# Splitting the second projection and the third residual of a fused attention block into column halves

## The reference

```
x = x + 0.5 * ffn(layernorm(x))
x = x + attn(layernorm(x))
x = x + 0.5 * ffn(layernorm(x))

ffn(u)  = u @ sign(weight).T
attn(u): Q = phi(u @ Wq.T + bq); K = phi(u @ Wk.T + bk); V = u @ Wv.T + bv     (16 heads of 64)
         KV = sum over n of K^T V;  Z = sum over n of K
         out = (Q KV) / (Q Z + eps);  return out @ Wo.T + bo
phi(a) = elu(a) + 1
```

## Time and profile before

| | us |
|---|---|
| median of three executions | 2138.48 |
| lowest and highest of them | 2082.67, 2271.7 |
| the profiled execution | 2096.74 |
| span of its slowest core, core 7 | 2095.1 |
| spans of the other seven cores | 2070.2 to 2080.0 |

### The profile page before, as it was taken

One profiled execution on the slowest core, in us unless ns is written; L12 is line 12 of the kernel. 1 busy time (PEld: TensorE's weight loads), 2 busy tenths in 40 slices (PEclk: granted clock), 3 DMA queues, 4 the chain that ended last, 5 costly groups with the idle time before them and its releaser, 6 DMA issues.

```text
span 2095.1 us, 33065 instructions; the slowest of 8 cores (2070.2 to 2095.1 us)
## 1 busy us (share of the span) xinstructions
PE 1771.3 (85%) x10784; PEld 793.9 (38%) x10784; DVE 759.3 (36%) x2049; ACT 1230.2 (59%) x2025; POOL 147.5 (7%) x274
## 2 busy tenths in 40 slices
PE   0499898998998998989989999878888888888887
PEld 0233333333333333333333333334444444444443
DVE  2133333333333333333333333134434444444443
ACT  1467667767667777676776766634444444444443
POOL 1000000000000001000000000010110011011010
PEclk9999999999999999999999999989999999999999
DMA  8622222222222223222222221123332332333332
GB/s 180 122 86 69 88 66 88 89 66 88 89 66 87 79 76 118 77 76 89 65 87 81 75 88 56 60 86 117 126 116 111 127 116 111 126 116 113 125 120 83
DMA packets 134630, 199.34 MB, mean 95 GB/s; under 512 B 88384, under 2 KB 88384, under 8 KB 134464
## 3 DMA queue, kind: packets, MB, share of 16 engines
q0 software_dynamic: 32960, 109.08, 15.5%
q1 hardware_dynamic: 101504, 88.15, 13.5%
HBM read 104.87 MB, written 83.89 MB: 90 GB/s over the span
## 4 chain that ended last, share of the span: by engine, by line
PE 64%; ACT 20%; issue 9%; DVE 4%; DMA 3%; ACTq 1%; DVEq 0%; SPq 0%
PE pA L465 43%; PE pA L476 12%; PE pA L470 3%; DVE y3t L323 3%; ACT mnb L399 3%; ACT mxb L401 3%; PE pA L480 2%; ACT kbQ L387 2%; ACT eb L400 2%; ACT u2fm L437 2%; PE tpB L455 2%; ACT kbQ L388 1%; DMA y3t<-wfT 1%; DMA stg<-wfT 1%; ACT kbK L403 1%
## 5 line engine op out<-in xcount | busy, mean ns | idle before, releaser
L476 PE MATMUL pA<-wv,u1fm 128*128 128x512 bf16 x1024 | 258.0, 397 | 97.2 <-ACT kbK L403 97.2
L465 PE MATMUL pA<-wo,attnfm 128*128 128x512 bf16 x1024 | 235.4, 383 | 70.6 <-DVE y3t L323 57.6
L465 PE MATMUL pA<-sw,u2fm 128*128 128x512 bf16 x1024 | 231.2, 379 | 48.0 <-ACT u2fm L439 44.3
L476 PE MATMUL pA<-wk,u1fm 128*128 128x512 bf16 x1024 | 242.4, 379 | 18.3 <-ACT kbQ L387 18.3
L465 PE MATMUL pA<-sw,u0fm 128*128 128x512 bf16 x1024 | 235.1, 383 | 0.0
L465 PE MATMUL pA<-wq,u1fm 128*128 128x512 bf16 x1024 | 232.1, 380 | 0.0
L437 ACT COPY u2fm<-tpB 128x512 bf16<-128x512 bf16 x64 | 37.5, 586 | 298.2 <-PE tpB L455 298.2
L476 PEld LDWEIGHTS pA<-wv,u1fm 128*128 128x128 bf16 x1024 | 93.4, 100 | 222.1 <-issue 137.7
L384 ACT ACTIVATE u2b<-y1t 128x1024 bf16<-128x1024 f32 x63 | 66.6, 1058 | 185.2 <-DVE y1t L283 185.2
L314 DVE TENSOR_TENSOR phiQ<-eb,mxb 128x1024 bf16<-128x1024 bf16 x64 | 44.3, 692 | 344.6 <-ACT mxb L401 344.6
L465 PEld LDWEIGHTS pA<-wo,attnfm 128*128 128x128 bf16 x1024 | 96.6, 98 | 183.8 <-issue 80.4
(11 more groups left out here) (120 smaller groups left out, 2454.8 us busy)
## 6 DMA issues: line engine op xcount, KB each, us to landing
xt<-x SPq DMA_DIRECT2D x64, 512.0 KB, 3.9
y1scr<-y1t POOLq DMA_DIRECT2D x64, 512.0 KB, 3.9
y1in<-y1scr POOLq DMA_DIRECT2D x64, 512.0 KB, 3.6
out<-y3t SPq DMA_DIRECT2D x64, 512.0 KB, 2.6
qscr<-qfm POOLq DMA_DIRECT2D x64, 256.0 KB, 3.2
qfin<-qscr POOLq DMA_DIRECT2D x64, 256.0 KB, 3.8
qfm<-phiQ SPq DMA_TRANSPOSE x512, 2.3
stg<-wfT SPq DMA_DIRECT2D x4, 512.0 KB, 8.7
```

Source lines behind the costliest of these rows:

```text
L465: mm = e.matmul(dst[:, h*512:(h+1)*512], lhs_fm[:, c*P:(c+1)*P], w_sb[:, c, h*512:(h+1)*512], start=(c == 0), stop=(last and c == 7))
L476: mm = e.matmul(dst[:, h*512:(h+1)*512], lhs_fm[:, c*P:(c+1)*P], w_sb[:, c, h*512:(h+1)*512], start=(c == 0), stop=(last and c == 7))
```

## The change

FFN and Wo of stage 2 no longer go through `proj`. Each is written out with the column half h as the outer loop, so the first half of `pA2` is complete after 8 matmuls. `tFfn2` counts halves. L323 becomes two instructions of 512 columns, each waiting for its half and each counting in `vY3`. Wo waits for the `y3t` half of the bank that it is about to write. Each of the two products now waits once, ahead of its first matmul, for both half copies of its input (`sU2fm`, `sAttnfm`). Wo's bias matmul comes at the end of each half. Thresholds of `tFfn2` and `vY3` elsewhere are doubled.

```
@@ VectorE
-                    v.wait_ge(tFfn2, t - 2)
+                    v.wait_ge(tFfn2, 2 * t - 5)
                     if tf >= 2:
                         v.wait_ge(dY3o[tf % 2], 16 * (tf // 2))
-                    v.scalar_tensor_tensor(y3t[:, tf % 2, :], pA2[:, :], 0.5, y2t[:, tf % 2, :],
+                    v.scalar_tensor_tensor(y3t[:, tf % 2, 0:512], pA2[:, 0:512], 0.5,
+                                           y2t[:, tf % 2, 0:512],
+                                           ALU.mult, ALU.add).then_inc(vY3, 1)
+                    v.wait_ge(tFfn2, 2 * t - 4)
+                    v.scalar_tensor_tensor(y3t[:, tf % 2, 512:1024], pA2[:, 512:1024], 0.5,
+                                           y2t[:, tf % 2, 512:1024],
                                            ALU.mult, ALU.add).then_inc(vY3, 1)
@@ TensorE
                     if t > NT:
-                        e.wait_ge(vY3, t - 3)
-                    proj(e, u2fm[:, (t - 3) % 2, :], sw, pA2[:, :], None, tFfn2,
-                         cw=(sU2fm, 2 * t - 5))
+                        e.wait_ge(vY3, 2 * (t - 3))
+                    e.wait_ge(sU2fm, 2 * t - 4)
+                    for h in range(2):
+                        for c in range(8):
+                            mm = e.matmul(pA2[:, h*512:(h+1)*512],
+                                          u2fm[:, (t - 3) % 2, c*P:(c+1)*P],
+                                          sw[:, c, h*512:(h+1)*512], start=(c == 0),
+                                          stop=(c == 7))
+                        mm.then_inc(tFfn2, 1)
@@
-                    if t >= 3:
-                        e.wait_ge(vY3, t - 2)
-                    proj(e, attnfm[:, (t - 1) % 2, :], wo, pA2[:, :], bor, tWo,
-                         cw=(sAttnfm, 2 * t - 1))
+                    e.wait_ge(sAttnfm, 2 * t)
+                    for h in range(2):
+                        if t >= 3:
+                            e.wait_ge(vY3, 2 * t - 5 + h)
+                        for c in range(8):
+                            e.matmul(pA2[:, h*512:(h+1)*512],
+                                     attnfm[:, (t - 1) % 2, c*P:(c+1)*P],
+                                     wo[:, c, h*512:(h+1)*512], start=(c == 0), stop=False)
+                        mm = e.matmul(pA2[:, h*512:(h+1)*512], ones_row[0:1, :],
+                                      bor[0:1, h*512:(h+1)*512], start=False, stop=True)
+                    mm.then_inc(tWo, 1)
```

More of the change, by code:

```diff
@@ L186, in _ @@
                 s, j = t // NJ, t % NJ
-                e.wait_ge(vY3, t + 1)
+                e.wait_ge(vY3, 2 * (t + 1))
                 if t >= 2:
@@ L337, in _ @@
                     if 3 <= t <= NT + 2:
-                        v.wait_ge(vY3, t - 2)
+                        v.wait_ge(vY3, 2 * (t - 2))
                     v.wait_ge(tWo, t)
```

## The result

| | before | after |
|---|---|---|
| median of the executions, us | 2084.54 (10 runs) | 2119.93 (9 runs) |
| profiled execution, us | 2096.74 | 2125.11 |
| span of core 7 in it, us | 2095.1 | 2123.4 |
| after / before | | 1.0178, 95% interval 1.0165 to 1.0191 |

The changed kernel is 1.8% slower, 35 us by the medians. That is far outside the scatter of the measurement, though under 2%. The forecast was +27 us, 1.3%. By it the kernel before has 2077 to 2080 us and the changed one 2113.5, give or take 1 us.

What follows compares the result with a forecast made beforehand. The loop through `pA2` (Wo, `y2t`, FFN, `y3t`) was taken to bound, ScalarE's loop close behind; +0.42 us in 62 iterations gave +26.0, iterations 1 and 2 +1.4, together +27.4: 2124.1 us, range 2094 to 2156.

Steps and rivals of the forecast that it cites:

- What ends late next: Ahead of Wo in stage 2: with `y3t` halved its wait goes, and the second `attnfm` copy holds Wo instead.
- The copy term: Ahead of Wo: waiting for the second `attnfm` copy starts Wo at 1606.27 against 1606.05, +0.22 us per Wo.
- The order of the matmuls in Wo: Wo up to the transposes: a second pair of changes between full and one-row bias matmuls costs +0.20 us.
- The rival of a free order: Wo's new matmul order costs nothing, so only the copy wait adds: +14.6 us, 2111 us; chance 0.12.
- FFN costed at nothing: Ahead of FFN: waiting for the second `u2fm` copy adds 0.13 us, off the loop that ends last, so no cost.
- the other three terms: Per iteration: forecast +0.22 (copy) and +0.20 (Wo's order), plus 0.12, the measured 0.26 us release delay against the forecast 0.14.
- The step that failed: Ahead of Wo: from the second `attnfm` copy's end to the matmul it released was taken as 0.14 us.
- The clock rival: TensorE's clock drops in some iterations, each costing 2.4 us; one in five gives 2153 us; chance 0.09.
- The saved wait: Ahead of Wo: ScalarE's loop does not bind, TensorE's sequence does; period 10.45 us, -43 us, 2054 us; chance 0.04.

Runs made afterwards that it cites:

- B: The kernel before the change, against which the changed kernel is compared: median 2084.54 us, period 11.17 us.

## Why the prediction was right or wrong

*What ends late next* was right. `y3t` went as a wait, the second `attnfm` copy took its place, and the time rose. The runs with the first copy alone (-29 us) and with the copies early (-92) show it from both sides.

*The copy term*, +0.22 us per iteration over B, is confirmed by the 29 us of moving Wo to the first copy: 0.49 us between the copies, less the 0.27 by which the first would have let Wo start sooner in B.

*The order of the matmuls in Wo*, +0.20, is confirmed twice (-12.6 and -15 us), and its place is as said. The rival of a free order falls as a rival for Wo with a bias behind each half, while the half order alone was free, and FFN, without biases, keeps its even pitch. The section of the Trainium skill that the prediction cites (TensorE: Matmul & The Clock Gate, "Wait — 56ns, not 53.3ns?") speaks of back-to-back matmuls and does not take up such a change among them.

*FFN costed at nothing* was right: its wait grew from 0.73 to 0.86 us, and the other three terms alone make up the 0.54 us of the usual iteration. It came into the price only after the copies had been moved.

*The step that failed* is the release delay in the sum: "plus 0.14". It was read at K's projection, where TensorE has a single wait ahead of the matmul. The trace of before showed 0.25 us at the two very waits that were to be replaced, and I put that down to VectorE as the releaser and let it go with it. It belonged to the pair of waits and their order. The changed kernel has such a pair ahead of Wo too, with the late one in front again, and there the delay measured 0.26 us; with the two waits exchanged it was 0.14. That is 0.12 us x 62, 7 us of the 8 between +27 and +35. The pair and its order stood in the listing of TensorE's program ahead of the prediction ("waits sAttnfm,vY3" for Wo). Because of it the effect is 1.8% instead of 1.3, near the 2% up to which I had counted the outcome as no change, with a chance of 0.83. That 2% was too wide for this measurement: its interval is 0.13% to either side, and the kernel is plainly slower.

*The clock rival* falls. From 1400 to 2070 us the granted clock on core 7 is 1.00 in both kernels, the 2.4 GHz level, and FFN's 16 matmuls take 3.61 us.

*The saved wait* falls as stated, and its condition is shown: with the copies early the period is 10.32 us, near the 10.45 that the rival gave, and the kernel is faster by 2.6%.

## What to carry to other kernels

Before a wait is removed, work out when every other operand of the same instruction is ready, and follow that chain round the loop; here 0.27 us was all that removing it could gain until ScalarE's copies were moved. In this kernel splitting a product paid where the consumer could start on the part that was ready, and one-row bias matmuls were cheaper together at the end. Where a TensorE instruction waits for several semaphores, try the one that comes last at the end of the list.

## What the runs showed that was not expected

A satisfied wait is not free on TensorE when it stands behind the one that ended last: 0.25 to 0.26 us from release to matmul in that order, 0.14 to 0.15 with the late one last, with ScalarE or VectorE as the releaser alike. In the kernel before, the order alone was worth 8 us by the period and 9 by the middle span. No run has more than two waits ahead of one matmul in its loop, so whether a third costs as much again stays open.

A few iterations have a VectorE instruction start about 0.35 us late after TensorE's release: L348 after a wait of 4.15 us in place of 3.79, as in the rows at 1615.35 and 1603.31 above. The same kind shows in the kernel before, at L323. No run here tries its cause.
